# A vision tower on one Trainium2 core: each head's own block of the values is picked on VectorE instead of by a padded projection

## The chip, the cores and the metric

The kernel runs on one core of a Trainium2 chip. A core has TensorE (PE, matmuls, with a weight load PEld that overlaps them), VectorE (DVE), ScalarE (ACT), GpSimd (POOL) and SyncE (SP), which here only issues DMA transfers. The engines run side by side and wait for each other by semaphores. The metric is the device time of one launch in microseconds; lower is better. Before the change it is 1733.34 us, the median of three runs (1732.08 to 1734.09).

## What is computed

The input is 4 x 64 x 64 tokens of 64 channels. Five layers follow, each but the first on a layer norm of `h` and added to it: windowed attention with rotary positions, local attention, a feed-forward net with routed experts, a decayed linear attention, and a gated binary layer. The change is in the second, the local attention:

```python
qkv = (x @ W_qkv.T).reshape(Bb, Nn, 3, NUM_HEADS, HEAD_DIM)      # 8 heads of 8 channels
attn = jnp.einsum('bhqd,bhkd->bhqk', q, k) * (scale * temperature[0])
attn = jnp.where(mask[None, None, :, :], attn, -jnp.inf)         # 7 x 7 neighbours on the 64 x 64 grid
attn = jax.nn.softmax(attn, axis=-1)
out = jnp.einsum('bhqk,bhkd->bhqd', attn, v)
out = jnp.transpose(out, (0, 2, 1, 3)).reshape(Bb, Nn, C)
return out @ W_proj.T + b_proj
```

## The kernel before

The program is written engine by engine. Each engine has its own list of instructions, in the order in which the code stands, and `wait_ge` on named semaphores holds an engine until others have come so far; no planner reorders anything. The helper `strips_ahead` runs the local stage: a front, then 64 strips of 256 tokens, the middle ones in a hardware loop with an even and an odd strip in its body. Each strip also does the layer norm and the query, key and value matmuls (called pre) of a strip five ahead.

In strip i TensorE does, in this order: the scores of the first half (L795, L799; a half is 4 of 8 patches of 16 queries), the row maxima's matmuls of strip i+1, first half (`peak`, L772, L776), the transposition of the normalized rows (L744), the projection of strip i-1 (`project`, L838), the pre values (L752), the scores and the maxima of the second halves, `values` of the first half, the pre keys and queries (L760), the transposition of the maxima (L784), and `values` of the second half. `values` makes the sums of the exponentials (L818, 16 matmuls, into the bank OT) and the weighted values (L824, 16 matmuls, into the bank AV).

The weighted values come for four heads at once. The 128 rows of AV are 2 groups of queries x 64 channels, and its 512 columns are 4 heads x 128 queries: each channel is weighted by the probabilities of all four heads of its half, of which only one is its own. VectorE's `weigh` takes the reciprocal of the sums (L1355) and multiplies all 512 columns by it, into `aT1` (L1358). The projection throws the foreign blocks away: its weights `w_p2` stand four times, each time with zeros in all channels but one head's, and four matmuls with these are added up.

In strip i VectorE does: the maxima of strip i+1, first half (`maxima`, L1350, two reductions), the addition of the projection of strip i-1 to `h` (`residual`, L1364), the moments of the rows six strips ahead (up to L1237 `veps_pre`), the maxima of the second half, the scaling of the pre queries (L1342), and `weigh(i)`. GpSimd waits for `veps_pre`, raises it to the power -1/2 (L528), and then makes the operands of strip i+2: the masked queries (L553, `q_block`) and two copies of the keys (L561, L562, `k_patch`), and adds the bias (L546). `peak` of that strip waits for `q_block` and `k_patch`. The projection waits for `attn_out` (L1358), the residual for `proj` (L838). ScalarE does the exponentials (L1146) and empties the banks of the pre matmuls.

Of the kernel before, what the change touches and what calls it, by code (L numbers as in the profile page):

```python
# [11 lines left out]
ALU = mybir.AluOpType  # L12
# [3 lines left out]
P = 128  # L16
B, H, W, C = 4, 64, 64, 64
NH, HD = 8, 8
# [7 lines left out]
NKL = KS * KS  # L26
# [31 lines left out]
def shape_tables():  # L58

    t = {}  # L60
# [13 lines left out]
    own = (np.arange(P)[:, None] == np.arange(P)[None, :] + 2 * HD) & (use < 2)[None, :]  # L74
# [3 lines left out]
    row = np.arange(P)  # L78
    t["q_mask"] = ((row % C // HD)[:, None] == np.arange(NH)[None, :]).astype(np.float32)
    t["ones_h"] = np.broadcast_to(np.arange(4)[:, None] == np.arange(32)[None, :] // HD, (P, 4, 32)).astype(np.float32)  # L80

    keys = np.zeros((2, C, 8, KS, KS), np.float32)
    for x in range(2):
        for n in range(8):
# [20 lines left out]
    i = np.arange(P, dtype=np.float64)  # L105
# [17 lines left out]
def build(nc, a, out):  # L123
    ctx = ExitStack()
    with ctx:
        def sb(name, shape, dt=F32):
            return ctx.enter_context(nc.sbuf_tensor(name, shape, dt))
# [4 lines left out]
        bank = {n: ctx.enter_context(nc.psum_tensor("ps_" + n, [P, 512], F32)) for n in ("T", "J1", "AV", "OT")}  # L132
# [8 lines left out]
        q_mask, ones_h = sb("q_mask", [P, NH]), sb("ones_h", [P, 4, 32])  # L141
# [5 lines left out]
        w_p1_rows, b_v1, bias1 = sb("w_p1_rows", [P, 2, C]), sb("b_v1", [P, P]), sb("bias1", [P, C])  # L147
        key_shift, head_row = sb("key_shift", [P, P]), sb("head_row", [P, 2])
        top_rows, ones_32 = sb("top_rows", [P, 4, P]), sb("ones_32", [P, 2, 32])
        w_kq2, w_v2, w_p2, bias2 = sb("w_kq2", [P, P]), sb("w_v2", [P, C]), sb("w_p2", [P, 4, C]), sb("bias2", [P, C])  # L150
        temp = sb("temp", [P, 1])
        w_i, b_i = sb("w_i", [P, HID]), sb("b_i", [P, 1])
        experts = sb("experts", [P, NLAY, NEXP + 1, HID + 1])
        shared = sb("shared", [P, NLAY, HID + 1])
# [14 lines left out]
        prob1, rec1, aT1 = sb("prob1", [P, 4, 512]), sb("rec1", [P, 256]), sb("aT1", [P, 512])  # L169
# [6 lines left out]
        rec2 = sb("rec2", [P, P])  # L176
# [41 lines left out]
        def named(prefix, *names):  # L218
            return {n: sem(prefix + "_" + n) for n in names}

        def times(count, most=None):


            if isinstance(count, int):
                return max(min(count, most) if most else count, 0) + 1
            return count + 1
# [3 lines left out]
        def settle(eng):  # L230

            eng.sem_inc(s_settled, 1)
# [1 line left out]
        T1 = named("tok", "x_in0", "x_in1", "qk_ps", "rope_mul", "rope", "k_ps", "k_sb", "v_ps", "v_sb", "max_ps", "max_done", "top_ps", "top_sb",  # L234
                   "scores", "exp_done", "av_done", "rec_done", "attn_out", "proj", "h_done")
        T2 = named("loc", "q_in0", "q_in1", "k_in0", "k_in1", "edge_in0", "edge_in1", "v_in0", "v_in1", "q_block", "k_patch", "max_ps", "max_done", "maxT", "negmax",
                   "scores", "exp_done", "av_done", "rec_done", "attn_out", "proj", "h_done")
        L = named("pre", "stats", "mv", "veps", "rstd", "minus_mean", "shift", "xn", "xT_ps", "xT_sb", "kq_ps", "v_ps", "k_sb", "q_sb", "v_sb", "stored0", "stored1",
                  "padded", "biased")
        FF = named("ffn", "stats", "mv", "veps", "rstd", "xn", "xT_ps", "xT_sb", "w_in", "hid_ps", "hid_sb", "biased", "out_ps", "h_done")  # L240
# [7 lines left out]
        def credited(count):  # L248

            return count + 1 + CREDIT  # L250
# [11 lines left out]
        def rows_of(x):  # L262

            return slice(C * x, C * (x + 1))
# [89 lines left out]
        def _(sp):  # L354
# [3 lines left out]
            later = [(q_mask[:, :], a["q_mask"]), (ones_h[:, :, :], a["ones_h"]), (q_rows[:, :], a["q_rows"]), (m_sb[:, :], a["m_init"]),  # L358
                     (decay[:, :], a["decay"]), (decay_q[:, :], a["decay_q"]), (key_rows[:, 0, :], a["key_rows"]),
                     (key_rows[:, 1, :], a["key_rows"]), (decay_k[:, :], a["decay_k"]), (w_kq2[:, :], a["w_kq2"]), (w_v2[:, :], a["w_v2"]),  # L360
                     (w_p2[:, :, :], a["w_p2"]), (bias2[:, :], a["b_p2"].broadcast_to((P, C))), (temp[:, :], a["temp"].broadcast_to((P, 1))),
                     (w_i[:, :], a["w_i"]), (b_i[:, :], a["b_i"]), (shared[:, :, :], a["shared"]), (w_o[:, :], a["w_o"]),
                     (b_o[:, :], a["b_o"].broadcast_to((P, C))), (w_qT[:, :], a["w_qT"]), (w_kT[:, :], a["w_kT"]), (w_v3[:, :], a["w_v3"]),
                     (w_gate[:, :], a["w_gate"]), (b_gate[:, :], a["b_gate"]), (lane_mask[:, :], a["lane_mask"]), (spread_f[:, :], a["spread"]),
# [242 lines left out]
        def _(pe):  # L607
# [195 lines left out]
            def values(j, par, g):  # L803
                i = j * 2 + par
                if g == 0:
                    pe.wait_ge(T2["v_in%d" % par], times((j + 1) * 48))
                    pe.wait_ge(T2["attn_out"], times(i))
                    pe.wait_ge(L["v_sb"], times(made(j, par)))
                pe.wait_ge(T2["exp_done"], times(i * 4 + 2 * g + 2))
                settle(pe)  # L810
                sums = bank["OT"][:, 0:P].rearrange("m (r p c) -> m p r c", r=QP, c=QP)
                attn = bank["AV"][:, :].rearrange("m (a r p c) -> m p a r c", a=4, r=QP, c=QP)
                for hd in range(4):
                    for x in range(2):
                        for e in range(2):
                            m = slice(32 * (2 * x + e), 32 * (2 * x + e + 1))
                            at = prob1[0:NKL, 2 * g + x, :].rearrange("k (p h r c) -> k h p r c", p=4, h=NH, r=QP)[:, 4 * e + hd, :, :, :]
                            pe.matmul(sums[m, 4 * g:4 * g + 4, :, :], ones_h[0:NKL, hd, :], at, start=hd == 0, stop=hd == 3)  # L818
                for u in range(4):
                    for x in range(2):  # L820
                        for e in range(2):
                            m = slice(32 * (2 * x + e), 32 * (2 * x + e + 1))
                            at = prob1[0:NKL, 2 * g + x, u * P + C * e:u * P + C * (e + 1)].rearrange("k (a r c) -> k a r c", a=4, r=QP)
                            mm = pe.matmul(attn[m, 4 * g + u, :, :, :], v_patch[:, par, 8 * x + 4 * g + u, 32 * e:32 * (e + 1)], at, start=True, stop=True)  # L824
                mm.then_inc(T2["av_done"], 1)

            def project(i, taken):
                pe.wait_ge(L["k_sb"], times(taken))
                pe.wait_ge(L["q_sb"], times(taken))
                pe.wait_ge(T2["attn_out"], times(i + 1))  # L830
                pe.wait_ge(T2["h_done"], times(i))
                settle(pe)
                for t in range(2):
                    for a4 in range(4):
                        for r in (2 * t, 2 * t + 1):
                            for x in range(2):
                                at = C * (r % 2) + 32 * x
                                mm = pe.matmul(bank["J1"][at:at + 32, t * C:(t + 1) * C], aT1[rows_of(x), a4 * P + 32 * r:a4 * P + 32 * (r + 1)],  # L838
                                               w_p2[rows_of(x), a4, :], start=a4 == 0, stop=a4 == 3)
                mm.then_inc(T2["proj"], 1)  # L840

            def front():
# [382 lines left out]
        def _(dve):  # L1225
# [125 lines left out]
                                      AX.X, ALU.max).then_inc(T2["max_done"], 1)  # L1351

            def weigh(i):
                dve.wait_ge(T2["av_done"], credited((i + 1) * 2))
                dve.reciprocal(rec2[:, :], bank["OT"][:, 0:P]).then_inc(T2["rec_done"], 1)  # L1355
                dve.wait_ge(T2["rec_done"], times(i + 1))
                dve.wait_ge(T2["proj"], times(i))
                dve.tensor_tensor(aT1[:, :].rearrange("m (a n) -> m a n", a=4), bank["AV"][:, :].rearrange("m (a n) -> m a n", a=4),  # L1358
                                  rec2[:, :].rearrange("m (a n) -> m a n", a=1).broadcast_to((P, 4, P)), ALU.mult).then_inc(T2["attn_out"], 1)

            def residual(i):
                dve.wait_ge(L["biased"], times(i + 1))
# [138 lines left out]
            staggered(dve, strips)  # L1501


NFIRST, NLATER, NFIRST_CONST = 12, 32, 7
NSTRIP = TOK // 256
NCONST = 18

# [57 lines left out]
```

## Time and profile before

| | |
|---|---|
| median of three runs | 1733.34 us |
| the profiled execution | 1728.17 us |
| its span, first to last instruction | 1726.4 us |
| mean granted TensorE clock over the span | 0.978 |
| token stage, then local stage, then the three last layers | about 0 to 360, 360 to 925, 925 to 1726 us |
| TensorE, VectorE, GpSimd busy in 380 to 860 us | 465, 304, 268 of 480 us |

The profiled execution is one execution with the hardware profiler. The tables of stretches tell which engine is busy when, the timeline what it does and what ended its idle time: `[0.47 <-PE ps_D L776]` behind a row means that the engine stood idle for 0.47 us before it, until L776 on TensorE was done. "issue" means that the profile names no releaser.

### The profile page before, as it was taken

How to read it: one execution, taken by the hardware profiler on the slowest of the kernel's cores; microseconds unless marked ns; L12 is line 12 of the kernel's file. 1: busy time of each engine (PE TensorE's matmuls, PEld its weight loads, DVE VectorE, ACT ScalarE, POOL GpSimd, SP SyncE). 2: the span in 40 equal slices, each digit the busy share in tenths (PEclk: the TensorE clock that was granted, in tenths of full speed). 3: DMA queues.
4: the chain of work that ended last, by engine and by line, in shares of the span. 5: the costliest groups of instructions: out<-in, count | busy, mean ns of one | idle time of the engine just before them, and what ended most of it. 6: DMA issues, size and time to landing. Idle time of an engine off the chain costs nothing.

```text
span 1726.4 us, 87999 instructions
## 1 busy us (share of the span) xinstructions
PE 1590.4 (92%) x32618; PEld 1205.7 (70%) x32618; DVE 1205.9 (70%) x3509; ACT 969.9 (56%) x1893; POOL 539.3 (31%) x699
## 2 busy tenths in 40 slices
PE   6898998779999999999996799999999999999996
PEld 4666676557888888888875566766666676666663
DVE  3887878746666666666654777787788778778762
ACT  1333333244444444444432477888888788888867
POOL 3311111054555555555541221222222222222210
PEclk9999999969999999999997899999999999999998
DMA  5101010034444444444431233333333333333332
GB/s 161 29 24 30 24 30 24 13 94 117 117 117 117 117 118 117 117 117 118 121 107 30 53 86 84 83 84 87 84 83 88 83 84 85 86 83 82 90 75 59
DMA packets 134691, 143.29 MB, mean 83 GB/s; under 512 B 42498, under 2 KB 90114, under 8 KB 134370
## 3 DMA queue, kind: packets, MB, share of 16 engines
q1 hardware_dynamic: 126306, 116.16, 25.9%
q10 hardware_dynamic: 8320, 26.22, 5.4%
q8 instruction: 46, 0.75, 0.2%
q14 instruction: 19, 0.16, 0.0%
HBM read 66.51 MB, written 16.99 MB: 48 GB/s over the span
## 4 chain that ended last, share of the span: by engine, by line
PE 81%; DVE 6%; issue 5%; SPq 3%; ACT 3%; DMA 1%; POOL 1%; DVEq 0%; ACTq 0%; POOLq 0%
PE ps_D L888 11%; PE ps_D L799 8%; PE ps_OT L818 4%; PE ps_J L838 4%; PE ps_D L676 3%; PE ps_AV L824 3%; PE ps_AV L905 3%; SPq L463 3%; PE ps_D L795 3%; PE ps_J L760 2%; PE ps_OT L752 2%; DVE tile_a L1286 2%; PE ps_J L996 2%; ACT prob L1176 2%; PE ps_J L964 2%
## 5 line engine op out<-in xcount | busy, mean ns | idle before, releaser
L1176 ACT ACTIVATE prob<-ps_D 128x1024 bf16<-128x1024 f32 x448 | 459.4, 1029 | 123.7 <-PE ps_D L888 122.1
L1146 ACT ACTIVATE prob<-ps_D 100x512 f32<-100x512 f32 x256 | 138.8, 594 | 219.2 <-PE ps_D L799 219.2
L1350 DVE TENSOR_REDUCE m_sb<-ps_D 128x4 f32<-128x400 f32 x256 | 135.4, 570 | 90.1 <-PE ps_D L776 90.0
L799 PE MATMUL ps_D<-tile_a,key_patch 64*100 64x128 f32 x2048 | 173.3, 287 | 0.6 <-issue 0.6
L888 PE MATMUL ps_D<-tile_b,w_parts 128*128 128x256 bf16 x1024 | 150.8, 272 | 14.2 <-DVE xg L1472 4.5
L888 PE MATMUL ps_D<-tile_a,w_parts 128*128 128x256 bf16 x1024 | 153.2, 276 | 9.5 <-ACT prob L1176 3.0
L799 PEld LDWEIGHTS ps_D<-tile_a,key_patch 64*100 64x100 f32 x2048 | 135.3, 165 | 0.8 <-issue 0.8
L553 POOL TENSOR_TENSOR tile_a<-q_st,q_mask 128x1024 f32<-128x1024 f32 x64 | 123.4, 1928 | 22.3 <-PE ps_D L799 10.6
L528 POOL TENSOR_TENSOR rstd_bin<-veps_bin,minus_half 128x2 f32<-128x2 f32 x64 | 44.1, 688 | 269.4 <-DVE veps_bin L1237 269.4
L795 PE MATMUL ps_D<-mT,key_rows 64*100 64x128 bf16 x1024 | 121.0, 226 | 7.8 <-issue 7.4
L528 POOL TENSOR_TENSOR rstd_ret<-veps_ret,minus_half 128x2 f32<-128x2 f32 x64 | 46.5, 727 | 250.8 <-DVE veps_ret L1237 250.8
L888 PEld LDWEIGHTS ps_D<-tile_b,w_parts 128*128 128x128 bf16 x1024 | 91.9, 102 | 46.7 <-issue 36.3
L888 PEld LDWEIGHTS ps_D<-tile_a,w_parts 128*128 128x128 bf16 x1024 | 93.6, 103 | 42.2 <-issue 30.7
L501 POOL TENSOR_TENSOR rot<-t_cos,t_sin 128x512 f32<-128x512 f32 x32 | 40.5, 1267 | 261.0 <-DVE t_sin L1279 261.0
L1435 DVE TENSOR_SCALAR prob<-ps_D 128x1024 bf16<-128x1024 f32 x64 | 78.4, 1225 | 59.7 <-PE ps_D L888 59.7
L528 POOL TENSOR_TENSOR rstd_pre<-veps_pre,minus_half 128x2 f32<-128x2 f32 x64 | 44.8, 700 | 227.0 <-DVE veps_pre L1237 227.0
L905 PE MATMUL ps_AV<-prob,lane_sum 128*32 128x256 bf16 x2048 | 103.4, 279 | 1.2 <-ACT prob L1176 1.2
L1472 DVE TENSOR_TENSOR xg<-ps_D,gates 128x1024 bf16<-128x1024 f32 x64 | 78.4, 1224 | 36.7 <-DMA tile_a<-xg 21.2
L1355 DVE RECIPROCAL rec<-ps_OT 128x128 f32<-128x128 f32 x64 | 61.3, 958 | 47.2 <-PE ps_AV L824 47.2
L1309 DVE TENSOR_REDUCE top<-ps_D 128x8 f32<-128x512 f32 x128 | 79.5, 684 | 15.8 <-PE ps_D L654 15.8
L1071 ACT ACTIVATE top_T<-ps_D 128x128 bf16<-128x128 f32 x32 | 8.9, 277 | 142.1 <-PE ps_D L663 142.1
L1078 ACT ACTIVATE prob<-ps_D 128x512 f32<-128x512 f32 x128 | 66.1, 603 | 35.9 <-PE ps_D L676 35.9
(176 smaller groups left out, 3976.8 us busy)
## 6 DMA issues: line engine op xcount, KB each, us to landing
tile_a<-xg SPq DMA_DIRECT2D x384, 64.0 KB, 2.0
tile_b<-xg SPq DMA_DIRECT2D x384, 64.0 KB, 2.0
key_st<-k_d SPq DMA_DIRECT2D x128, 162.0 KB, 3.1
tile_b<-v_d ACTq DMA_DIRECT2D x128, 120.0 KB
tile_b<-v_d ACTq DMA_DIRECT2D x64, 160.0 KB
w_exp<-experts SPq DMA_DIRECT2D x64, 129.0 KB, 2.3
xT<-in_x SPq DMA_DIRECT2D x32, 256.0 KB, 2.7
k_d<-kpad SPq DMA_DIRECT2D x64, 64.0 KB, 2.9
```

What stands on the lines that cost most here:

```text
L528: gp.tensor_tensor(rstd[:, :], veps[:, :], minus_half[:, 0:veps.shape[1]], ALU.pow).then_inc(q["rstd"], 1)
L553: gp.tensor_tensor(q_block[:, par, :].rearrange("c (p h q) -> c p h q", h=NH, q=NQ), q_st[:, par, :].rearrange("c (p a q) -> c p a q", a=1 ...
L795: pe.matmul(s_loc[x][0:NKL, u * P:(u + 1) * P], top_half(key_rows[rows_of(x), par, at * NKL:(at + 1) * NKL]), mT[rows_of(x), par, :], star ...
L799: mm = pe.matmul(s_loc[x][0:NKL, u * P:(u + 1) * P], key_patch[rows_of(x), par, at * NKL:(at + 1) * NKL], q_block[rows_of(x), par, at * P: ...
L888: mm = pe.matmul(d[:, a * 512 + oh * 256:a * 512 + (oh + 1) * 256], w_parts[:, at, oh, :, :].rearrange("r i o -> r (i o)"), x_parts[half][ ...
L905: mm = pe.matmul(bank["AV"][32 * cg:32 * (cg + 1), 0:256], lane_sum[:, int(k == 1), :], sgn[:, k % 4, cg * 256:(cg + 1) * 256], start=k == ...
L1146: act.activation(prob1[0:NKL, 2 * g + x, :], s_loc[x][0:NKL, :], ACT.Exp).then_inc(T2["exp_done"], 1)
L1176: act.activation(sgn[:, k % 4, :], unit(k, par)[:, :], ACT.Sign).then_inc(BN["sign"], 1)
L1309: dve.tensor_reduce(top1[:, j, 0:NH], s_tok[j][:, :].rearrange("q (w k) -> q w k", k=NKT), AX.X, ALU.max).then_inc(T1["max_done"], 1)
L1350: dve.tensor_reduce(m_sb[:, C * x + HOT[x] + 4 * g:C * x + HOT[x] + 4 * g + 4], m_loc[x][:, 0:4 * NKL].rearrange("p (u n) -> p u n", u=4), ...
L1435: dve.tensor_scalar(sgn[:, 1, :], unit(1, par)[:, :], -TINY, TINY, ALU.max, ALU.min).then_inc(BN["clip"], 1)
L1472: dve.tensor_tensor(xg[:, :].rearrange("r (n t) -> r n t", n=4), ring(5, par)[:, :].rearrange("r (n t) -> r n t", n=4), gates[:, :].rearra ...
```

## The change

Three edits in the local stage, and what they need.

`weigh` on VectorE now makes one 128 x 128 block out of the four: the first head's block of AV times a column of ones and zeros (`head_mask[:, 0]`, a one in the channels of that head), then three times the next head's block times its column plus what is there. The block is then multiplied by the reciprocal. Each of these five waits for the one before. The projection takes 8 matmuls with the plain weights, where there were 32. And the reciprocal waits for a new semaphore, `sums`, which TensorE raises behind the last matmul of the sums, and no longer for the values behind them.

```diff
@@ values (TensorE)
-                            pe.matmul(sums[m, 4 * g:4 * g + 4, :, :], ones_h[0:NKL, hd, :], at, start=hd == 0, stop=hd == 3)
+                            mm = pe.matmul(sums[m, 4 * g:4 * g + 4, :, :], ones_h[0:NKL, hd, :], at, start=hd == 0, stop=hd == 3)
+                if g:
+                    mm.then_inc(T2["sums"], 1)
@@ project (TensorE)
-                    for a4 in range(4):
-                        for r in (2 * t, 2 * t + 1):
-                            for x in range(2):
-                                at = C * (r % 2) + 32 * x
-                                mm = pe.matmul(bank["J1"][at:at + 32, t * C:(t + 1) * C], aT1[rows_of(x), a4 * P + 32 * r:a4 * P + 32 * (r + 1)],
-                                               w_p2[rows_of(x), a4, :], start=a4 == 0, stop=a4 == 3)
+                    for r in (2 * t, 2 * t + 1):
+                        for x in range(2):
+                            at = C * (r % 2) + 32 * x
+                            mm = pe.matmul(bank["J1"][at:at + 32, t * C:(t + 1) * C], aT1[rows_of(x), 32 * r:32 * (r + 1)], w_p2[rows_of(x), :], start=True, stop=True)
@@ weigh (VectorE)
+                dve.wait_ge(T2["sums"], times(i + 1))
+                dve.reciprocal(rec2[:, :], bank["OT"][:, 0:P]).then_inc(T2["rec_done"], 1)
                 dve.wait_ge(T2["av_done"], credited((i + 1) * 2))
-                dve.reciprocal(rec2[:, :], bank["OT"][:, 0:P]).then_inc(T2["rec_done"], 1)
+                dve.wait_ge(T2["proj"], times(i))
+                settle(dve)
+                for hd in range(4):
+                    src, own = bank["AV"][:, hd * P:(hd + 1) * P], head_mask[:, hd:hd + 1]
+                    if hd == 0:
+                        dve.tensor_scalar(aT1[:, 0:P], src, own, None, ALU.mult).then_inc(T2["picked"], 1)
+                    else:
+                        dve.wait_ge(T2["picked"], times(i * 4 + hd))
+                        settle(dve)
+                        dve.scalar_tensor_tensor(out=aT1[:, 0:P], in0=src, scalar=own, in1=aT1[:, 0:P], op0=ALU.mult, op1=ALU.add).then_inc(T2["picked"], 1)
                 dve.wait_ge(T2["rec_done"], times(i + 1))
-                dve.wait_ge(T2["proj"], times(i))
-                dve.tensor_tensor(aT1[:, :].rearrange("m (a n) -> m a n", a=4), bank["AV"][:, :].rearrange("m (a n) -> m a n", a=4),
-                                  rec2[:, :].rearrange("m (a n) -> m a n", a=1).broadcast_to((P, 4, P)), ALU.mult).then_inc(T2["attn_out"], 1)
+                dve.wait_ge(T2["picked"], times(i * 4 + 4))
+                settle(dve)
+                dve.tensor_tensor(aT1[:, 0:P], aT1[:, 0:P], rec2[:, :], ALU.mult).then_inc(T2["attn_out"], 1)
@@ tables
+    t["head_mask"] = ((row % 32 // HD)[:, None] == np.arange(4)[None, :]).astype(np.float32)
-    part = (np.arange(C) // HD % 4)[:, None, None] == np.arange(4)[None, :, None]
-    arr["w_p2"] = np.tile(np.where(part, n(L0_attn_W_proj).T[:, None, :], np.float32(0.0)), (2, 1, 1))
+    arr["w_p2"] = np.tile(n(L0_attn_W_proj).T, (2, 1))
```

On VectorE, in the hardware loop of the local stage, an odd strip ended like this before (`q_sb` the pre queries, `rec` the reciprocal, `ps_OT` the sums, `ps_AV` the values, `aT` what the projection reads, `m_sb` the next strip's maxima):

```order
L1341 ISA [waits pre_kq_ps]
L1342 TENSOR_SCALAR q_sb<-ps_J,temp 64x256 [waits pre_stored1]
L1354 REGISTER_ALU
L1355 RECIPROCAL rec<-ps_OT 128x128 [waits loc_av_done]
L1358 TENSOR_TENSOR aT<-ps_AV,rec 128x512 [waits loc_proj,loc_rec_done]
```

and now ends like this:

```order
L1343 ISA [waits pre_kq_ps]
L1344 TENSOR_SCALAR q_sb<-ps_J,temp 64x256 [waits pre_stored1]
L1357 RECIPROCAL rec<-ps_OT 128x128 [waits loc_sums]
L1358 REGISTER_ALU
L1364 TENSOR_SCALAR aT<-ps_AV,head_mask 128x128 [waits loc_av_done,loc_proj]
L1366 ISA
L1368 SCALAR_TENSOR_TENSOR aT<-ps_AV,head_mask,aT 128x128 [waits loc_picked]
L1366 REGISTER_ALU
L1368 SCALAR_TENSOR_TENSOR aT<-ps_AV,head_mask,aT 128x128 [waits loc_picked]
```

Two more rows like the last two follow, one more accumulation with its register step, and the multiplication L1372. The reciprocal has stayed in its place among VectorE's instructions; what it waits for has moved forward on TensorE.

On TensorE, around the projection, from the last scores of the first half, before:

```order
L772 MATMUL ps_D<-key_rows,q_rows 128x400 [waits loc_max_done,loc_edge_in0,loc_q_block,loc_k_patch]
L772 MATMUL ps_D<-key_rows,q_rows 128x400
L776 MATMUL ps_D<-key_patch,tile_a 128x100 x8
L838 MATMUL ps_J<-w_p,aT 32x64 [waits loc_h_done,loc_attn_out,pre_k_sb,pre_q_sb]
L838 MATMUL ps_J<-w_p,aT 32x64 x31
L795 MATMUL ps_D<-mT,key_rows 100x128 [waits loc_exp_done]
```

and now:

```order
L774 MATMUL ps_D<-key_rows,q_rows 128x400 [waits loc_max_done,loc_edge_in0,loc_q_block,loc_k_patch]
L774 MATMUL ps_D<-key_rows,q_rows 128x400
L778 MATMUL ps_D<-key_patch,tile_a 128x100 x8
L841 MATMUL ps_J<-w_p,aT 32x64 [waits loc_h_done,loc_attn_out,pre_k_sb,pre_q_sb]
L841 MATMUL ps_J<-w_p,aT 32x64 x7
L797 MATMUL ps_D<-mT,key_rows 100x128 [waits loc_exp_done]
```

These rows are from one of the last strips, which have no pre work any more; in the others the rows' transposition stands in front of the projection and the pre values behind it. Only the number of projection matmuls differs, 8 for 32.

## Rows read from the trace of the kernel before

**Rows 1.** The page: busy time of the engines, and the chain by engine.

```profile
PE 1590.4 (92%) x32618; PEld 1205.7 (70%) x32618; DVE 1205.9 (70%) x3509; ACT 969.9 (56%) x1893; POOL 539.3 (31%) x699
PE 81%; DVE 6%; issue 5%; SPq 3%; ACT 3%; DMA 1%; POOL 1%; DVEq 0%; ACTq 0%; POOLq 0%
```

**Rows 2.** Stretches: length, PE, PEld, DVE, ACT, POOL busy, clock, DMA share, GB/s.

```profile
380.00:860.00 480.00, 465.24 (x14929) 394.11 (x14925) 303.58 (x781) 218.62 (x555) 268.40 (x333) 1.00 0.43 118
```

**Rows 3.** Timeline of two strips: start us, duration us, engine, line, operation, [idle before].

```profile
606.93 0.35 PE L772 MATMUL ps_D<-key_rows,q_rows 64*128 64x400 bf16 x2 [0.19 <-issue]
...
607.59 1.06 DVE L1350 TENSOR_REDUCE m_sb<-ps_D 128x4 f32<-128x400 f32 x2 [0.47 <-PE ps_D L776]
...
607.74 1.10 PE L838 MATMUL ps_J<-w_p,aT 64*32 64x64 f32 x64
...
608.76 0.69 PE L752 MATMUL ps_OT<-w_v,xnp 128*128 128x64 f32 x4
609.10 0.29 DVE L1364 TENSOR_TENSOR h<-ps_J,h 128x128 f32 x1 [0.45 <-PE ps_J L838]
...
610.39 0.70 POOL L528 TENSOR_TENSOR rstd_pre<-veps_pre,minus_half 128x2 f32<-128x2 f32 x1 [3.40 <-DVE veps_pre L1237]
...
612.87 0.65 PE L818 MATMUL ps_OT<-prob,ones_h 100*32 100x64 f32 x32
612.98 0.49 DVE L1342 TENSOR_SCALAR q_sb<-ps_J,temp 64x256 f32<-64x256 f32 x1 [0.71 <-PE ps_J L760]
...
613.34 0.63 PE L824 MATMUL ps_AV<-prob,tile_b 100*32 100x64 f32 x32
...
614.04 0.96 DVE L1355 RECIPROCAL rec<-ps_OT 128x128 f32<-128x128 f32 x1 [0.57 <-PE ps_AV L824]
...
614.05 1.01 POOL L562 COPY key_patch<-key_st 128x480 f32<-128x480 f32 x1
...
615.03 0.69 DVE L1358 TENSOR_TENSOR aT<-ps_AV,rec 128x512 f32<-128x512 f32 x1
...
615.47 0.37 PE L772 MATMUL ps_D<-key_rows,q_rows 64*128 64x400 bf16 x2
...
616.15 1.06 DVE L1350 TENSOR_REDUCE m_sb<-ps_D 128x4 f32<-128x400 f32 x2 [0.43 <-PE ps_D L776]
...
616.30 1.10 PE L838 MATMUL ps_J<-w_p,aT 64*32 64x64 f32 x64
...
617.68 0.29 DVE L1364 TENSOR_TENSOR h<-ps_J,h 128x128 f32 x1 [0.47 <-PE ps_J L838]
...
622.73 1.02 POOL L562 COPY key_patch<-key_st 128x480 f32<-128x480 f32 x1
...
624.11 0.35 PE L772 MATMUL ps_D<-key_rows,q_rows 64*128 64x400 bf16 x2 [0.21 <-issue]
```

**Rows 4.** Timeline of VectorE: first and last residual of the steady strips.

```profile
411.54 0.29 DVE L1364 TENSOR_TENSOR h<-ps_J,h 128x128 f32 x1 [0.47 <-PE ps_J L838]
...
866.64 0.29 DVE L1364 TENSOR_TENSOR h<-ps_J,h 128x128 f32 x1 [0.45 <-PE ps_J L838]
```

**Rows 5.** VectorE by form, kernel up to 925 us: xcount | busy us, mean ns.

```profile
L1286 DVE TENSOR_SCALAR tile_a<-ps_T,head_row 128x256 f32<-128x256 f32 x64 | 28.0, 480 | 52.4 <-PE ps_T L632 52.4
L1278 DVE SCALAR_TENSOR_TENSOR t_cos<-ps_T,b_qk,cos 128x512 f32<-128x512 f32 x32 | 23.8, 744 | 2.3 <-PE ps_J L625 2.3
L1342 DVE TENSOR_SCALAR q_sb<-ps_J,temp 64x256 f32<-64x256 f32 x61 | 29.9, 490 | 46.9 <-PE ps_J L760 46.9
L1364 DVE TENSOR_TENSOR h<-ps_J,h 128x128 f32 x56 | 16.4, 292 | 25.5 <-PE ps_J L838 25.5
```

**Rows 6.** Timeline of the stage's last strips.

```profile
898.21 0.69 DVE L1358 TENSOR_TENSOR aT<-ps_AV,rec 128x512 f32<-128x512 f32 x1
...
899.12 0.87 PE L838 MATMUL ps_J<-w_p,aT 64*32 64x64 f32 x47 [0.22 <-issue]
...
922.72 1.93 PE L838 MATMUL ps_J<-w_p,aT 64*32 64x64 f32 x64 [1.95 <-issue]
```

More of the change, by code:

```diff
@@ L149, in build @@
         top_rows, ones_32 = sb("top_rows", [P, 4, P]), sb("ones_32", [P, 2, 32])
-        w_kq2, w_v2, w_p2, bias2 = sb("w_kq2", [P, P]), sb("w_v2", [P, C]), sb("w_p2", [P, 4, C]), sb("bias2", [P, C])
-        temp = sb("temp", [P, 1])
+        w_kq2, w_v2, w_p2, bias2 = sb("w_kq2", [P, P]), sb("w_v2", [P, C]), sb("w_p2", [P, C]), sb("bias2", [P, C])
+        temp, head_mask = sb("temp", [P, 1]), sb("head_mask", [P, 4])
         w_i, b_i = sb("w_i", [P, HID]), sb("b_i", [P, 1])
@@ L236, in build @@
         T2 = named("loc", "q_in0", "q_in1", "k_in0", "k_in1", "edge_in0", "edge_in1", "v_in0", "v_in1", "q_block", "k_patch", "max_ps", "max_done", "maxT", "negmax",
-                   "scores", "exp_done", "av_done", "rec_done", "attn_out", "proj", "h_done")
+                   "scores", "exp_done", "sums", "av_done", "rec_done", "picked", "attn_out", "proj", "h_done")
         L = named("pre", "stats", "mv", "veps", "rstd", "minus_mean", "shift", "xn", "xT_ps", "xT_sb", "kq_ps", "v_ps", "k_sb", "q_sb", "v_sb", "stored0", "stored1",
@@ L360, in _ @@
                      (key_rows[:, 1, :], a["key_rows"]), (decay_k[:, :], a["decay_k"]), (w_kq2[:, :], a["w_kq2"]), (w_v2[:, :], a["w_v2"]),
-                     (w_p2[:, :, :], a["w_p2"]), (bias2[:, :], a["b_p2"].broadcast_to((P, C))), (temp[:, :], a["temp"].broadcast_to((P, 1))),
+                     (w_p2[:, :], a["w_p2"]), (head_mask[:, :], a["head_mask"]), (bias2[:, :], a["b_p2"].broadcast_to((P, C))), (temp[:, :], a["temp"].broadcast_to((P, 1))),
                      (w_i[:, :], a["w_i"]), (b_i[:, :], a["b_i"]), (shared[:, :, :], a["shared"]), (w_o[:, :], a["w_o"]),
@@ L1501, in _ @@
             staggered(dve, strips)
-NFIRST, NLATER, NFIRST_CONST = 12, 32, 7
+NFIRST, NLATER, NFIRST_CONST = 12, 33, 7
 NSTRIP = TOK // 256
```

## The prediction, made before the changed kernel ran

> **What bounds the kernel now.** I read the page first: TensorE is busy for 92% of the span, VectorE for 70%, and 81% of the chain that ended last is TensorE [rows 1]. The edit touches only the local attention stage, so the whole-kernel shares say little; the stretches by time say more. From 380 to 860 us TensorE is busy 465 of 480 us at the full granted clock (2.4 GHz), VectorE 304, GpSimd 268 [rows 2]. That looks like a TensorE stage. But a chain of work can make an engine look like the bound when another one releases it just in time, so I then read the timeline of two strips, an even one and an odd one [rows 3].
>
> The stage has 64 strips. Between the residual additions (L1364) at 411.54 and at 866.64 lie 53 of them, 8.587 us each [rows 4]. In the timeline TensorE idles at two places in two strips only, one of them 0.19 to 0.21 us in front of the row-maximum matmuls of the first half (L772) in every second strip. The page calls it "issue". The GpSimd rows say otherwise: L562, the last key copy, ends at 622.73+1.02 = 623.75, and L772 starts at 624.11, 0.36 later; in the other strip the copy ends at 615.06 and L772 starts at 615.47, 0.41 later [rows 3]. L772 waits for that copy. So GpSimd is on the path although it is 56% busy in this stage, and it forms a loop:
>
> L772 (maxima matmuls) → VectorE L1350 → projection L838 → VectorE residual L1364 → moments → GpSimd L528, then its masking and two copies → next L772.
>
> GpSimd itself idles 3.40 us per strip until VectorE's moments come, and these stand behind the residual, and the residual behind the projection [rows 3]. Two strips take 624.11-606.93 = 17.18; without the idle 0.2 TensorE's own order takes 16.98, 8.49 a strip. The loop over GpSimd is 17.18 less the 0.05 by which the copy came early in one of the two strips, 8.57 a strip. Two paths with almost the same length; an edit must shorten both.
>
> **The change, part by part.**
>
> *Projection.* 32 matmuls (64 records, two for each in float32) start at 607.74, and the next matmuls (L752) at 608.76: 1.02 us, 16 ns a record [rows 3]. 8 matmuls are 16 records, 0.26 us. Both paths lose 0.77 us if nothing else steps in. If the few records expose a start or an end of about one record (0.22 us), it is 0.55; I take 0.77, since L752 starts before the last record of L838 ends at 608.84.
>
> *VectorE, the reciprocal.* Now it starts at 614.04, behind the last value matmul, 613.34+0.63 = 613.97, so a signal costs 0.07. The sums (L818) end at 612.87+0.65 = 613.52; the query scaling in front of it on VectorE ends at 612.98+0.49 = 613.47 [rows 3]. So it starts at 613.59 and ends at 614.55. The value matmuls have ended by then, so the new first wait costs nothing, and nothing useful stood behind the reciprocal that could be late. It gains 0.45.
>
> *VectorE, the picks.* One multiplication of 128x512 (0.69 us) becomes four operations of 128x128 that read the values in PSUM and a column, and one multiplication of 128x128 in SBUF. The trace has no such shape. From below: L1364, 128x128 with PSUM but without a column, 0.292. Forms with a column: L1286 (256 elements from PSUM) 0.480, L1278 (512 elements) 0.744 [rows 5]. These two rows lie 0.264 apart for 256 elements, 1.03 ns an element, so 128 elements come to 0.348 from either. From above: L1342, 64x256 from PSUM with a column and a strided pattern, 0.490 [rows 5]. I take 0.35, since both contiguous forms give it, and 0.29 for the last multiplication. A dependent operation starts 0.03 after its forerunner (615.03 against 615.00). Sum: 4 x 0.38 + 0.29 = 1.80, from 614.58 to 616.38, where the old form ended at 615.72. The weighing ends 0.66 later. Counted from the start of the second half's sums (612.87) it ends at 3.51 instead of 2.85.
>
> The Trainium skill, page "VectorE: DVE Perf Modes", section on the TRN2 errata, prices a PSUM-to-SBUF operation at 120 cycles plus one per element at 0.96 GHz, which for 128 elements is an estimated 0.258 us. The rows with a column disagree (256 elements: 0.480 here, 0.392 by the page). By the page the weighing would be some 0.37 shorter, and loop 2 below 7.72 instead of 8.09.
>
> *Who waits for the later end.* Queued behind the weighing on VectorE are the maxima of the next strip (L1350), and TensorE's projection waits for it. Both have to be held against the new, shorter strip.
>
> **Loop 1, over GpSimd.** The projection would be done 0.77 earlier, but VectorE can't add the residual at once: it is in the maxima until 607.59+1.06 = 608.65. So the residual starts at 608.68, not at 609.10: 0.42 gained; in the other strip 616.15+1.06+0.03 = 617.24 against 617.68: 0.44. In that strip GpSimd was not yet the last (0.41 against 0.36): 0.05 more. Of the 17.18 for two strips 0.91 goes: 16.27, which is 8.13 a strip. So 0.31 of the 0.77 is lost behind the maxima.
>
> **Loop 2, over the picks.** Sums start → weighing ends 3.51 → projection starts 0.22 later (the weighing ended at 898.90 and the projection started at 899.12 where it did wait [rows 6]) → sums start again: 612.87-607.74 = 5.13, less 0.77 = 4.36. Together 8.09. Before, it was 2.85+0.22+5.13 = 8.20, hidden under 8.59. So it would lie just under loop 1, with 0.04 to spare. TensorE's own order would need 8.49-0.77 = 7.72 and waits for the rest.
>
> The maxima don't wait for the weighing: L772 comes 8.13-5.17 = 2.96 after the sums' start, its maxima 0.66 later at 3.62, and the weighing ends at 3.51.
>
> **The sum.** Steady strips: 53 x (8.587-8.13) = 24.2 us. Three strips before them lie in the same loops: 1.2. In the last seven the projection already waits for the weighing [rows 6], so +0.66-0.77 = -0.1 each: 0.7. The very last projection takes 1.93 us where others take 1.10 [rows 6]; a quarter of the records saves three quarters of it, 1.4, the picks cost 0.66: 0.8. Together 26.9 us. From the profiled execution's 1728.17 this is 1701.3. The median of the runs is 1733.34, 5.2 above it, so I forecast 1733.3-26.9 = 1706.4, say 1706.5. Smaller weights and one more 2 KB load at the start lie beside the token stage: nothing.
>
> **The rivals.** 0.2%, 3.5 us, is about what can be told from no change.
>
> A, as forecast, loop 1 holds: saves 20 to 30 us. For it: two rows of unlike length give the same VectorE price. 0.58.
>
> B, the picks or a drained projection hold: picks of 0.40 instead of 0.35 (the register steps between them not hidden), or 0.2 of the projection exposed, lengthen loop 2 to some 8.30. Saves 53 x 0.29 = 15 and nothing in the last strips: 1718. For it: 0.04 is a thin cover. 0.22.
>
> C, TensorE alone sets the pace at 7.72: 53 x 0.87 = 46 and 2 in the rest: 1685. Both loops would have to be wrong, against the constant 0.36 behind the copy. 0.05.
>
> D, GpSimd's key copy is slowed. L562 would run from 1.6 to 2.6 after the sums' start, while the accumulating picks run from 2.1 on, with two operands in SBUF (the accumulator and the column). If the copy stood still in the overlap, 0.5 us, loop 1 would be 8.63, and the kernel 1733 to 1736. The trace has L562 at 1.01 with no such neighbour. 0.05. The Trainium skill, page "GPSIMD Engine Reference", section Specifications, says that GpSimd's SBUF interfaces are shared with VectorE and contended by instructions with two SBUF inputs; no row of this stage shows it either way.
>
> E, slower. Picks at L1342's 0.490 add 4 x 0.14 = 0.56 to loop 2: 8.65, 0.06 above now, so 53 x 0.06 = 3, and 0.56-0.1 in each of the last seven, another 3: 1740. It decides from picks of 0.47 on. 0.07.
>
> F, something that I don't see takes the gain (the SP queue's stores, instruction fetch): 1732. No row speaks for it. 0.03.
>
> **How the numbers follow.** Faster by over 0.2%: A, B, C and a little of F, 0.86. Slower: E and a third of D, 0.08. The rest 0.06. The range goes from 1697 (a little more than A's end) to 1722 (into B); outside are C, most of D, E and F.
>
> **What would show it.** Right: L838 with 16 records and some 0.26 us to L752; picks of about 0.35; the residual starting 0.03 behind the maxima, with no idle time; L772 idle 0.3 to 0.5 in every strip, 0.36 behind the copy; 8.1 to 8.2 us a strip. Wrong: the projection starting 0.2 behind the last multiplication in each strip (B, or E where picks are long); L562 well above 1.02 (D); strips of 7.7 (C).

## The result: no gain, 0.3% slower

| | before | after |
|---|---|---|
| median of 14 runs each | 1731.99 us | 1735.97 us |
| ratio | | 1.003, 95% interval 1.002 to 1.004 |
| the profiled execution, its span | 1728.17, 1726.4 us | 1738.07, 1736.3 us |
| one strip of the steady part of the local stage | 8.587 us | 8.674 us |

The forecast was 1706.5 us, in a range of 1697 to 1722. The profiled execution of after is one of its slower ones, and that of before one of the faster; behind the last local residual the unchanged layers took 1736.3 - 928.51 = 807.8 us in the one and 801.6 in the other. So the causes are read from the strips, and the sizes from the medians: 53 x (8.674 - 8.587) = 4.6 us, against 4.0 measured. One of the 14 runs of after took 2078.67 us at a granted clock of 0.648 and stands outside the ratio; the median of the other 13 is 1735.70.

The page of after, busy time by engine and the chain by engine:

```profile
PE 1554.3 (90%) x29546; PEld 1167.1 (67%) x29546; DVE 1258.4 (72%) x3765; ACT 974.2 (56%) x1893; POOL 539.1 (31%) x699
PE 71%; issue 10%; DVE 5%; ACT 4%; SPq 4%; POOL 3%; DMA 1%; ACTq 0%; DVEq 0%; POOLq 0%
```

The stretch of [rows 2], with the same columns:

```profile
380.00:860.00 480.00, 428.26 (x12219) 355.96 (x12207) 348.56 (x994) 220.22 (x551) 268.34 (x333) 1.00 0.43 117
```

TensorE lost 465.24 - 428.26 = 37.0 us of work in this stretch, and none of it became time: TensorE stands idle instead. On the page its part of the chain fell from 81% to 71% and "issue" doubled [rows 1]. Where it idles, the waits of after in the same stretch say (us in total, times, longest):

```profile
PE ps_J L841 <- issue: 29.8, 55, 1.1
...
PE ps_D L774 <- POOL key_patch L564: 13.3, 26, 0.5
```

It idles in front of the projection (L841) in all 55 strips, which it did in neither strip of [rows 3]. The wait for GpSimd's copy, the path that the forecast thought the longest, is left in every second strip. The timeline of one strip and the edge of the next shows the loop that took over:

```profile
600.54 0.29 DVE L1372 TENSOR_TENSOR aT<-aT,rec 128x128 f32<-128x128 f32 x1
...
601.04 0.43 PE L841 MATMUL ps_J<-w_p,aT 64*32 64x64 f32 x16 [0.68 <-issue]
601.17 1.06 DVE L1352 TENSOR_REDUCE m_sb<-ps_D 128x4 f32<-128x400 f32 x2 [0.34 <-issue]
...
605.50 0.65 PE L820 MATMUL ps_OT<-prob,ones_h 100*32 100x64 f32 x32
...
606.23 0.96 DVE L1357 RECIPROCAL rec<-ps_OT 128x128 f32<-128x128 f32 x1
...
607.12 1.00 POOL L564 COPY key_patch<-key_st 128x480 f32<-128x480 f32 x1
...
607.22 0.35 DVE L1364 TENSOR_SCALAR aT<-ps_AV,head_mask 128x128 f32<-128x128 f32 x1
...
607.72 1.35 DVE L1368 SCALAR_TENSOR_TENSOR aT<-ps_AV,head_mask,aT 128x128 f32<-128x128 f32 x3
...
608.47 0.35 PE L774 MATMUL ps_D<-key_rows,q_rows 64*128 64x400 bf16 x2 [0.50 <-POOL key_patch L564]
...
609.21 0.29 DVE L1372 TENSOR_TENSOR aT<-aT,rec 128x128 f32<-128x128 f32 x1
...
609.72 0.43 PE L841 MATMUL ps_J<-w_p,aT 64*32 64x64 f32 x16 [0.36 <-issue]
...
610.07 0.68 PE L754 MATMUL ps_OT<-w_v,xnp 128*128 128x64 f32 x4
610.41 0.29 DVE L1377 TENSOR_TENSOR h<-ps_J,h 128x128 f32 x1
...
614.18 0.65 PE L820 MATMUL ps_OT<-prob,ones_h 100*32 100x64 f32 x32
```

The sums start at 605.50, and the weighing ends at 609.21 + 0.29 = 609.50: 4.00 later, where the forecast had 3.51. The projection follows at 609.72, 0.22 behind it as in [rows 6], and the next sums at 614.18, 4.46 behind the projection. Together 8.68. The first and last residual of an even number of steady strips, 52, give (862.31 - 411.25) / 52 = 8.674, for the 8.587 of [rows 4]:

```profile
411.25 0.28 DVE L1377 TENSOR_TENSOR h<-ps_J,h 128x128 f32 x1
...
862.31 0.28 DVE L1377 TENSOR_TENSOR h<-ps_J,h 128x128 f32 x1
```

The 4.00 doesn't come from the operations. By form in 380 to 860 us (xcount | busy us, mean ns | idle us before them, and what ended it) they are what was forecast:

```profile
L1368 DVE SCALAR_TENSOR_TENSOR aT<-ps_AV,head_mask,aT 128x128 f32<-128x128 f32 x167 | 58.5, 351 | 24.5 <-DVE aT L1368 0.2 <-DVE aT L1364 0.2
...
L1364 DVE TENSOR_SCALAR aT<-ps_AV,head_mask 128x128 f32<-128x128 f32 x56 | 19.6, 351 | 2.1 <-PE ps_AV L828 0.3
...
L1372 DVE TENSOR_TENSOR aT<-aT,rec 128x128 f32<-128x128 f32 x55 | 16.0, 292 | 8.1
```

The picks take 0.351 (forecast 0.35), the multiplication 0.292 (0.29). But in front of L1368 stand 24.5 / 167 = 0.147 us of idle time each, and in front of L1372 8.1 / 55 = 0.147, where the forecast charged 0.03. The view names hardly any releaser for them, so they are easily read past. Four times 0.12 is 0.48, the whole difference between 3.51 and 4.00. The first pick also has the extra instruction described below, but its waits were met long before: it starts at 607.22, 0.03 behind the reciprocal's end at 607.19.

### The profile page after: what moved, and what is told of

It is laid out like the page before. It is cut to its first block, busy times and chain, and to the rows that moved or that the text cites. A ratio compares the mean times of both kernels' runs of the same rounds, so it can differ in the third digit from the quotient of the medians.

```text
span 1736.3 us, 82594 instructions
## 1 busy us (share of the span) xinstructions
PE 1554.3 (90%) x29546; PEld 1167.1 (67%) x29546; DVE 1258.4 (72%) x3765; ACT 974.2 (56%) x1893; POOL 539.1 (31%) x699
## 4 chain that ended last, share of the span: by engine, by line
PE 71%; issue 10%; DVE 5%; ACT 4%; SPq 4%; POOL 3%; DMA 1%; ACTq 0%; DVEq 0%; POOLq 0%
PE ps_D L890 11%; PE ps_D L801 6%; PE ps_D L678 3%; SPq L465 3%; PE ps_AV L907 3%; PE ps_OT L820 2%; PE ps_OT L754 2%; PE ps_J L998 2%; PE ps_D L797 2%; DVE tile_a L1288 2%; PE ps_J L966 2%; PE ps_J L948 2%; PE ps_OT L644 2%; PE ps_J L1029 2%; PE ps_T L626 2%
## 5 line engine op out<-in xcount | busy, mean ns | idle before, releaser
L1352 DVE TENSOR_REDUCE m_sb<-ps_D 128x4 f32<-128x400 f32 x256 | 135.2, 570 | 64.1 <-PE ps_D L778 54.8
L1368 DVE SCALAR_TENSOR_TENSOR aT<-ps_AV,head_mask,aT 128x128 f32<-128x128 f32 x192 | 67.3, 351 | 28.2 <-DVE aT L1368 0.5
```

Of the source, the lines that this page charges most:

```text
L1352: dve.tensor_reduce(m_sb[:, C * x + HOT[x] + 4 * g:C * x + HOT[x] + 4 * g + 4], m_loc[x][:, 0:4 * NKL].rearrange("p (u n) -> p u n", u=4), ...
```

## The experiments

The strips in the text are measured as above, over an even number of them. Each timed run is compared with the kernel before on the same chip.

**Settling taken out.** The accumulating picks and the multiplication each wait for a semaphore, and between wait and operation the code issues `settle`, an instruction of its own that only raises a semaphore, so that the wait is held by it and not by the operation. Here the operation holds the wait itself; the first pick keeps its settle.

```diff
                         dve.wait_ge(T2["picked"], times(i * 4 + hd))
-                        settle(dve)
...
                 dve.wait_ge(T2["picked"], times(i * 4 + 4))
-                settle(dve)
```

> The changed kernel without the separate semaphore increment (settle) that stands between each wait on `picked` and the operation behind it; the waits stay. My theory: in the changed kernel each accumulating pick starts 0.15 us behind its forerunner and not 0.03, because the wait sits on that extra instruction; four such gaps make the weighing 0.48 longer than predicted and the loop over the picks 8.67 us a strip. Without them: gaps of 0.03, the weighing ends 3.5 after the start of the sums, strips of 8.15 to 8.2, kernel about 1710. Rival: the 0.15 is the price of reading what the operation before has just written in place; then the gaps stay at 0.15, strips at 8.67, kernel 1736.

1716.1 us (1713.6 to 1723.1), ratio 0.9917 (0.9888 to 0.9947); strips of 8.36. The timeline:

```profile
604.76 0.65 PE L820 MATMUL ps_OT<-prob,ones_h 100*32 100x64 f32 x32
...
605.49 0.96 DVE L1357 RECIPROCAL rec<-ps_OT 128x128 f32<-128x128 f32 x1
...
606.48 0.35 DVE L1364 TENSOR_SCALAR aT<-ps_AV,head_mask 128x128 f32<-128x128 f32 x1
...
606.86 1.12 DVE L1367 SCALAR_TENSOR_TENSOR aT<-ps_AV,head_mask,aT 128x128 f32<-128x128 f32 x3
...
609.18 0.66 PE L754 MATMUL ps_OT<-w_v,xnp 128*128 128x64 f32 x4 [0.23 <-ACT xnp L1099]
```

The first accumulation starts at 606.86, 0.03 behind the pick's end at 606.83, and three of them span 1.12 instead of 1.35. The weighing ends 3.55 after the sums' start. An instruction that computes nothing, run four times a strip, was worth 19.9 us between the medians (1735.97 and 1716.1).

**The same, in the kernel before.** One settle is put between the wait for the reciprocal and the multiplication, which before had 0.03 between them (614.04 + 0.96 to 615.03 in [rows 3]).

```diff
-                dve.wait_ge(T2["rec_done"], times(i + 1))
                 dve.wait_ge(T2["proj"], times(i))
+                dve.wait_ge(T2["rec_done"], times(i + 1))
+                settle(dve)
                 dve.tensor_tensor(aT1[:, :]...
```

> The kernel before with the extra semaphore increment (settle) between VectorE's wait for the reciprocal and the multiplication behind it, nothing else. My theory: the gap between the two grows from 0.03 to 0.15 us, in every strip; the strip stays at 8.59, since GpSimd's loop and not the weighing sets it there. Rival (the gap in the changed kernel came from the short picks or from working in place): it stays 0.03.

```profile
607.27 0.96 DVE L1355 RECIPROCAL rec<-ps_OT 128x128 f32<-128x128 f32 x1 [0.56 <-PE ps_AV L824]
608.37 0.69 DVE L1359 TENSOR_TENSOR aT<-ps_AV,rec 128x512 f32<-128x512 f32 x1
```

607.27 + 0.96 = 608.23 to 608.37: 0.14. The gap is made by the settle, in another kernel and in front of another operation. The one run took 1733.11 against a median of 1733.47 before, and its strips 8.59: there the weighing had room.

**Each edit alone.** The reciprocal alone, in the kernel before:

```diff
-                dve.wait_ge(T2["av_done"], credited((i + 1) * 2))
+                dve.wait_ge(T2["sums"], times(i + 1))
                 dve.reciprocal(rec2[:, :], bank["OT"][:, 0:P]).then_inc(T2["rec_done"], 1)
+                dve.wait_ge(T2["av_done"], credited((i + 1) * 2))
```

> The kernel before with one part of the change alone: the reciprocal waits for the sums. My theory: the loop over GpSimd (8.57) sets the strip, so an earlier reciprocal moves nothing in the steady strips; in the last seven the projection starts 0.45 earlier each. 1729 against 1732 for the kernel before. Rival (the weighing was on the path already before): 0.45 a strip, about 1705.

1730.91 us, ratio 1.000 (0.9987 to 1.0013); strips of 8.59. Alone it is worth nothing that can be told. The projection alone, in the kernel before (three in four heads are left out of the output):

```diff
-                    for a4 in range(4):
+                    for a4 in range(1):
...
-... start=a4 == 0, stop=a4 == 3)
+... start=True, stop=True)
```

> The kernel before with the short projection alone: 8 matmuls with the first of the four blocks; the contribution of three in four heads is left out. VectorE does its old work. My theory: this shows the loop over GpSimd by itself, the residual waiting for the maxima in front of it: 8.13 a strip, L562's end to L772 0.36 in every strip, kernel about 1732-0.455x56-7 = 1700. Rival (TensorE's own order sets the pace): 7.7 a strip, 1685.

1713.73 us, ratio 0.9905 (0.9888 to 0.9923); strips of 8.29. That is most of the forecast gain, but not the 8.13 that loop 1 gave. Its timeline says why:

```profile
602.06 0.43 PE L838 MATMUL ps_J<-w_p,aT 64*32 64x64 f32 x16
602.45 0.37 ACT L1097 ACTIVATE xnp<-ps_T 64x256 f32<-64x256 f32 x1
...
602.89 0.28 DVE L1364 TENSOR_TENSOR h<-ps_J,h 128x128 f32 x1
...
602.97 0.66 PE L752 MATMUL ps_OT<-w_v,xnp 128*128 128x64 f32 x4 [0.48 <-ACT xnp L1097]
```

Behind the short projection TensorE waits 0.48 us for ScalarE's copy of the turned rows (L1097), 0.57 in the next strip. The copy stands behind two exponentials, and the long projection had covered it. L772 comes 0.50 and 0.82 behind GpSimd's key copy here, not 0.36, so loop 1 has room: this third path, which is not in the forecast, holds the strip. The picks alone, with the changed kernel's picks and a projection of 32 matmuls again:

```diff
+                    for a4 in range(4):
...
-... aT1[rows_of(x), 32 * r:32 * (r + 1)], w_p2[rows_of(x), :], start=True, stop=True)
+... aT1[rows_of(x), 32 * r:32 * (r + 1)], w_p2[rows_of(x), a4, :], start=a4 == 0, stop=a4 == 3)
```

> The changed kernel with the projection at its old length: 32 matmuls, four times over the same picked block with the padded weights, so nothing is left out. My theory: the loop over the picks is 4.00+0.22+5.13 = 9.35 a strip, 0.76 above the kernel before, and the kernel about 1783. Rival (the picks are not what holds the strip): 8.6 to 8.7 a strip, 1732 to 1740.

1777.55 us, ratio 1.0268 (1.0244 to 1.0292); strips of 9.36. Loop 2 with the long projection was expected at 9.35: the picks alone cost 45 us, far more than the 18 that the projection alone gives.

**The reciprocal back behind the values, in the changed kernel:**

```diff
                 dve.wait_ge(T2["sums"], times(i + 1))
-                dve.reciprocal(...)
                 dve.wait_ge(T2["av_done"], credited((i + 1) * 2))
+                dve.reciprocal(...)
```

> The changed kernel with one part undone: the reciprocal waits for the values again and not for the sums. My theory: in the changed kernel the loop over the picks sets the strip, so the 0.45 by which the reciprocal starts later goes into each strip in full: 8.67+0.45 = 9.12, kernel about 1736+0.45x63 = 1764. Rival (another loop holds at 8.67): under 1745.

1776.7 us, ratio 1.025 (1.0233 to 1.0267). The usual strips are 9.12 (8.71 and 9.53 in turn), which is loop 2 with 0.45 more (8.67 + 0.45). The edit that was worth nothing alone is worth 40.7 us between the medians once its chain sets the pace. The strips' 0.45 make 24 of them and the clock some 11 (below); for the rest no run shows where it goes.

**The third path removed.** The experiment on the projection, and ScalarE copies the turned rows between the two exponentials of the first half instead of behind them:

```diff
-                weights(0)
+                weights(0, 0)
                 if m is not None:
                     pre_turned(m, 1 - par)
+                weights(0, 1)
```

> The projection-only kernel (three in four heads' contributions left out) with one edit on ScalarE: the copy of the transposed rows (xnp) stands between the two exponentials of the first half and no longer behind both. In the projection-only kernel the strips took 8.29 and not 8.13, and TensorE stood idle for 0.5 us a strip in front of the pre values (L752), released by that copy, which the long projection had hidden. My theory: that wait is the bound there; with the copy 0.6 earlier it goes, and the strips fall to 8.13 to 8.16, the loop over GpSimd, kernel about 1706. Rival (the GpSimd loop is itself 8.29 long): no change, 1714.

1700.69 us, ratio 0.982 (0.9801 to 0.9839); strips of 8.07. As three in four heads are missing, this is a bound and no kernel to use. The timeline:

```profile
600.91 0.37 PE L772 MATMUL ps_D<-key_rows,q_rows 64*128 64x400 bf16 x2
...
601.59 1.06 DVE L1351 TENSOR_REDUCE m_sb<-ps_D 128x4 f32<-128x400 f32 x2 [0.43 <-PE ps_D L776]
...
602.44 0.66 PE L752 MATMUL ps_OT<-w_v,xnp 128*128 128x64 f32 x4 [0.28 <-ACT xnp L1097]
...
602.56 0.28 DVE L1365 TENSOR_TENSOR h<-ps_J,h 128x128 f32 x1
...
607.57 1.01 POOL L562 COPY key_patch<-key_st 128x480 f32<-128x480 f32 x1
...
608.93 0.35 PE L772 MATMUL ps_D<-key_rows,q_rows 64*128 64x400 bf16 x2
...
610.36 0.65 PE L752 MATMUL ps_OT<-w_v,xnp 128*128 128x64 f32 x4 [0.20 <-ACT xnp L1097]
```

The wait for ScalarE is halved, not gone: 0.28 and 0.20 in turn, where it was 0.48 and 0.57. The 8.07 lies near the 8.13 of loop 1, but it isn't loop 1 alone. L772 follows the key copy by 0.35 (608.58 to 608.93) in every second strip, and there loop 1 takes 608.93 - 600.91 = 8.02. In the next strip L772 comes 0.54 behind the copy (616.51 to 617.05), so loop 1 has room there; what is left to hold it is TensorE's own order with the wait for ScalarE, 8.12.

**Versions that compute everything.** All start from the kernel without settling. One takes the moments ahead of the maxima and the residual on VectorE, one moves the ScalarE copy, one does both:

```diff
+                if more:
+                    pre_moments(nxt)
                 if not last:
                     maxima(i + 1, 0)
                 if not first:
                     residual(i - 1)
-                if more:
-                    pre_moments(nxt)
```

> The changed kernel without the extra increments in the picks, and with the moments in front of the first half's maxima and of the residual in VectorE's order, which cuts GpSimd's loop free of both. My theory: the kernel without the increments stood at 8.36 a strip, since in every odd strip the branch at the end of VectorE's loop (0.33) delayed maxima, residual and moments and so GpSimd; with GpSimd out of it the copy on ScalarE (8.29) or the picks (8.22) hold: about 8.3 a strip, 1713. Rival (the loop over the picks holds alone): no change, 1716; if the moments delay the maxima too much, slower, 1722.

> The changed kernel without the extra increments in the picks, and with the copy of the transposed rows between the two exponentials; VectorE's order as in the changed kernel. My theory: the loop over GpSimd, late by the branch of VectorE's loop in every odd strip (0.33), is then the one that holds there: 8.25 to 8.35 a strip, 1708 to 1714. Rival (the copy alone makes the odd strips long): 8.25, as with the moments first.

> The changed kernel without the extra increments in the picks, with the moments first on VectorE, and with the copy of the transposed rows between the two exponentials on ScalarE. My theory: three loops hold this stage. Over GpSimd (cut free by the moments' place), over ScalarE's copy (L754 waits for it, eased by its place), and over the picks: 3.55+0.24+4.46 = 8.25 a strip, which is then alone. Kernel about 1732-56x0.34-5 = 1708. Rival (the extra 0.23 in every odd strip of the kernel with the moments first is not the copy's): 8.36, 1715.

Moments first: 1714.87 us, ratio 0.9887 (0.987 to 0.9903), strips of 8.36. Copy moved: 1716.6, 0.9898 (0.9876 to 0.992), 8.365. Both: 1712.3 (1710.66 to 1717.06), 0.9878 (0.9858 to 0.9898), 8.31. Each move alone leaves the strip where it was: the projection still starts 0.21 to 0.27 behind the weighing in each strip, and every second time the way back to the sums stays longer, since the pre values wait 0.2 us for ScalarE. Both together have the lowest median, but the intervals of these three and of the kernel without settling overlap. In the timeline of both together the projection still waits for the weighing in each strip:

```profile
603.61 0.29 DVE L1371 TENSOR_TENSOR aT<-aT,rec 128x128 f32<-128x128 f32 x1
...
604.11 0.43 PE L841 MATMUL ps_J<-w_p,aT 64*32 64x64 f32 x16 [0.60 <-issue]
...
608.58 0.65 PE L820 MATMUL ps_OT<-prob,ones_h 100*32 100x64 f32 x32
...
611.84 0.29 DVE L1371 TENSOR_TENSOR aT<-aT,rec 128x128 f32<-128x128 f32 x1
...
612.34 0.43 PE L841 MATMUL ps_J<-w_p,aT 64*32 64x64 f32 x16 [0.26 <-issue]
...
612.49 0.37 DVE L1234 BATCH_NORM_STATS2 stats_pre<-h 128x6 f32 x2 [0.36 <-issue]
...
613.52 1.06 DVE L1353 TENSOR_REDUCE m_sb<-ps_D 128x4 f32<-128x400 f32 x2
...
614.73 0.36 PE L774 MATMUL ps_D<-key_rows,q_rows 64*128 64x400 bf16 x2
...
616.97 0.65 PE L820 MATMUL ps_OT<-prob,ones_h 100*32 100x64 f32 x32
```

The last attack on loop 2 puts the scores of the second half between the weighing and the projection, from the kernel with the moments first:

```diff
+                scores(j, par, 1)
                 if not first:
                     project(i - 1, ...)
                 if m is not None:
                     pre_values(m, 1 - par)
-                scores(j, par, 1)
```

> A version meant to be faster than both: the changed kernel without the extra increments, the moments first on VectorE, and on TensorE the scores of the second half in front of the projection and the pre values. The projection then has 1.3 us more to wait in for the picks, and the copy on ScalarE more time too. My theory: the loop over the picks shrinks to about 7, GpSimd's to 7.3, and TensorE's own order with its wait for the exponentials is left, 8.1 to 8.15 a strip: 56x0.45+5 = 30 us less than the kernel before, about 1702. Rival (ScalarE, which empties the pre values in front of the second half's exponentials, becomes late): 8.3 and more, 1712.

1749.85 us, ratio 1.0098 (1.0079 to 1.0117), strips of 8.91. The projection's wait is gone, and a longer one has come:

```profile
598.84 0.26 PE L797 MATMUL ps_D<-mT,key_rows 64*100 64x128 bf16 x2 [0.56 <-ACT prob L1148]
...
601.38 0.28 ACT L1105 ACTIVATE v_sb<-ps_OT 128x128 f32<-128x128 f32 x1 [2.42 <-PE ps_OT L754]
...
602.61 1.08 ACT L1148 ACTIVATE prob<-ps_D 100x512 f32<-100x512 f32 x2 [0.95 <-issue]
...
604.54 0.96 DVE L1357 RECIPROCAL rec<-ps_OT 128x128 f32<-128x128 f32 x1 [0.30 <-PE ps_OT L820]
```

TensorE waits 0.56 us for the first half's exponentials before it can make the scores of the second half. ScalarE's exponentials of that half stand behind its copy of the pre values (L1105), and those now come late: ScalarE idles 2.42 us for them, though the scores are done by 600.27 in the same timeline. Behind the copy 0.95 more passes, in which ScalarE's queue issues a DMA (L1135, 601.61 to 602.43). Which of the three makes how much of the 8.91 was not tried apart.

## Why the prediction was wrong

**The step that failed** is "A dependent operation starts 0.03 after its forerunner (615.03 against 615.00). Sum: 4 x 0.38 + 0.29 = 1.80". The 0.03 was read at a place whose wait rides on the operation. Four of the new places have a settle between a wait that is met only then and the operation, and there it is 0.15: taking it out of after gives 0.03, putting it into before gives 0.14. So the sum is 1.80 + 4 x 0.12 = 2.28, and 607.22 to 609.50 is 2.28. The trace of before had the price in a later stage, where moments wait for the residual through a settle (columns as in [rows 5], 925 to 1700 us):

```profile
L1231 DVE BATCH_NORM_STATS2 stats_ret<-h 128x6 f32 x108 | 19.1, 219 | 8.2 <-DVE h L1494 8.1
```

Two records for each of 54 passes: 8.1 / 54 = 0.15 each. The row to look for was the nearest in form of wait, not the nearest in place.

**Loop 2** was the right rival mechanism with a term too small: 8.09 plus 0.48 is 8.57, and 0.10 is in the return from projection to sums, 4.46 for 4.36. There the projection holds the next matmuls for 0.35 (609.72 to 610.07), not 0.26: what was forecast as a rival's 0.2 of exposed projection is half of that. Together 8.67, as measured. With a cover of 0.04 any such error decided the case; the forecast gave loop 2 a chance of 0.22 at 8.30 and 0.07 at 8.65, and bounded the operations' durations from both sides, but not the gaps between them. Rival E's size and sign were right, its cause (picks of 0.490) wrong.

**Loop 1** was the forecast's pace at 8.13, and it holds neither after nor the experiment on the projection. There the path over ScalarE holds the strip at 8.29, 0.30 of the 0.46 that loop 1 promised; so even picks without the extra gaps would not have given the forecast gain. That is the second error: the term "Both paths lose 0.77 us if nothing else steps in" named no cover for the shorter projection, and the copy behind the exponentials had been hidden by just this work. Loop 1 itself was put too long: the forecast let the residual start 0.03 behind the maxima. The residual needs nothing of theirs, and it starts 0.09 before their end (602.56, against 601.59 + 1.06 = 602.65, with the copy moved). That is 0.12 a strip, and 8.13 - 0.12 = 8.01 is the 8.02 measured there. So the nearness of 8.07 and 8.13 is luck: a loop that was put too long, and a wait that was left out.

Without the settling, loop 2 is 3.55 + 0.21 + 4.47 = 8.23 in one strip. In the next the pre values wait 0.23 for ScalarE's copy (609.18), the way back is 4.74 and the strip 8.50 (sums at 604.76 and 613.26). The mean is the measured 8.36.

**What held.** The reciprocal starts 606.23 - 605.50 = 0.73 after the sums (0.72 forecast). The picks and the multiplication last what the rows with a column gave. By the Trainium skill, page "VectorE: DVE Perf Modes", section on the TRN2 errata, a pick was an estimated 0.258; the trace has 0.351, so here the page is too low, as the row at 256 elements had said.

**Rival D** is refuted: the key copy L564 takes 1.00 beside the picks (607.12 to 608.12, over the pick and the first accumulation), and 1.00 to 1.03 in all its records from 411 to 860 us, as L562 before (1.00 to 1.02). The rule of the Trainium skill, page "GPSIMD Engine Reference", section Specifications, on contention with operations of two SBUF inputs shows no effect here, if an accumulator and a column count as the two. That is no test of two full tensors: L1372, which reads two of 128x128 from SBUF, runs while GpSimd is idle.

**The last strips.** The forecast saved 1.5 us in them. From the residual at 870.57 to the last at 928.51 after takes 57.9 us, and before, from 866.64 to 924.77, 58.1. No run tested them apart.

**What stays open.** The best version has strips of 8.31, for 8.07 with the plain multiplication. One of its strips is loop 2 with nothing on top, 3.55 + 0.21 + 4.47 = 8.23. The next is 8.39 (608.58 to 616.97): L774 of the second half starts at 614.73, 0.15 behind the maxima of the first half (613.52 + 1.06 = 614.58), for which the code lets it wait, and these stand behind the moments, which started 0.36 late. The two weren't tried apart, and 8.23 is the least from sums to sums in any version that computes everything.

## What to carry to other kernels

When an edit adds links to a dependent chain, price each gap from a row with the same form of wait, and look through the whole trace for one; four gaps of 0.12 us a strip cost 20 us here, more than the 16 that the edit gives without them. When an engine's work shrinks, list what ran under it on the other engines before booking the gain: of the 0.77 us that the projection lost, 0.5 came back as the next wait. An edit worth nothing alone (the reciprocal) can be worth 1 to 2% once another puts its chain on the critical path, so parts are judged in the state in which they will run.

## What the runs showed of the hardware

A dependent VectorE operation starts 0.03 to 0.04 us behind its forerunner if it holds the wait itself, and 0.14 to 0.15 us if a separate semaphore instruction holds it. If the wait was met before, the separate instruction adds nothing (607.19 to 607.22), and an operation that needs nothing of its forerunner started 0.09 us before that one's end (602.56 against 602.65).

In every second strip VectorE's first operation behind the hardware loop's branch starts 0.34 us late with its inputs ready (L1352 at 601.17, [0.34 <-issue]; L1372 had ended at 600.83). With the moments first it is their first operation that is late, by 0.36 (L1234 at 612.49), so the place in the loop makes the delay and not the operation. That the branch is what takes the time is argued from this place.

The clock was not expected to matter. With the late reciprocal TensorE idles 1.1 us in front of one projection and 0.8 in front of the next, and in seven of the steady strips the granted clock falls. One such place, in stretches of that kernel, with the columns of [rows 2]:

```profile
625.00:630.00 5.00, 3.68 (x60) 2.91 (x58) 4.33 (x13) 1.74 (x4) 1.70 (x3) 0.91 0.53 154
630.00:632.00 2.00, 2.00 (x24) 1.91 (x22) 0.25 (x3) 0.00 (x0) 0.90 (x2) 0.50 0.18 43
632.00:634.00 2.00, 2.00 (x78) 1.60 (x73) 1.06 (x2) 1.74 (x4) 1.75 (x1) 0.88 0.07 24
```

From 630 to 632 it is at 0.50, the 1.2 GHz level, and for a part of the stretches on both sides, though TensorE is busy all the time from 630 to 634. In the 5 us before, TensorE was busy for 3.68, with 0.53 us idle in front of L774 and 0.79 in front of the projection. The strip around it takes 11.1 us, where others of its kind take 9.5. In after, which idles 0.4 to 0.7 in front of its projections, the clock stays at 1.00 in this stage, and so it does with the picks alone (0.7 and 0.8). Of the 43 us by which that kernel is slower than before, loop 2 makes 53 x (9.12 - 8.587) = 28, and the seven strips 7 x 1.6 = 11. TensorE idles in front of every projection of that kernel; why the clock falls in some strips and not in others was not tried.
